# Cross-attention scores: two heads as 128 stationary columns instead of one head as 64

## The chip, the cores and the metric

One core of a Trainium2 chip runs the whole kernel in one launch. The metric is the device time of an execution in microseconds (us); lower is better. Times before and after are medians over executions. One execution was also recorded by the hardware profiler, and all rows below come from that one.

## The reference

One pre-norm decoder layer on 32 sequences of 64 tokens, 512 wide, all in float32: `x = x + self_attention(norm(x))`, `x = x + cross_attention(norm(x), ctx)`, `x = x + lora_linear(norm(x))`. Only the second step is touched. It has 32 query heads of 128 in 8 groups; the four query heads of a group share one key head and one value head:

```python
q = (query @ Wq).reshape(nb, q_len, H, D).transpose(0, 2, 1, 3)     # nb 32, q_len 64, H 32, D 128
k = (key @ Wk).reshape(nb, q_len, KVH, D).transpose(0, 2, 1, 3)     # KVH 8
v = (value @ Wv).reshape(nb, q_len, KVH, D).transpose(0, 2, 1, 3)
q = q * cos + _rotate_half(q) * sin
k = k * cos + _rotate_half(k) * sin
k = jnp.repeat(k, GROUPS, axis=1)                                   # GROUPS 4
v = jnp.repeat(v, GROUPS, axis=1)
scores = jnp.einsum('bhqd,bhkd->bhqk', q, k) / jnp.sqrt(jnp.float32(D))
scores = jnp.where(mask == 0, jnp.float32(-1000000000.0), scores)
attn = jax.nn.softmax(scores, axis=-1)
x = jnp.einsum('bhqk,bhkd->bhqd', attn, v)
return x.transpose(0, 2, 1, 3).reshape(nb, q_len, H * D) @ Wo
```

## The kernel before

The program is written engine by engine: each engine has its own list of work, in program order, and semaphores (`need`) tie the lists together. There is no planner; the order is the order of the code. Keys and values of the cross-attention are computed first and parked in device memory, then self-attention runs (to about 515 us), then cross-attention (about 515 to 1350 us), then the LoRA linear layer.

Cross-attention (`CrossAttention`) walks over `ITS` = 32 iterations: 8 groups of heads, and within each group 4 blocks of 512 tokens (8 sequences). One iteration is one group of four query heads (`h` = 0 to 3) on one block. `product3` (L68, matmuls at L75 to L77) and `output` (L1233 to L1235) build an accurate product out of three fast products (`F32R`, operands split into a high and a low part). The scores (L1194) and the transposes (L1205) are done on plain float32; a plain float32 product is recorded as two weight loads (LDWEIGHTS) and two matmuls.

TensorE's own list in the steady loop of `rest()` is, for iteration `it`: `mix(it, 0)`, `mix(it, 1)` (attention times values, L1220), `scores(it + 1)` (L1194), `queries(it + 2, 0)` (L75 to L77, 12 matmuls), `output(it, 0)` (L1233 to L1235, 12 matmuls), `queries(it + 2, 1)`, `output(it, 1)`, `turn(it + 1, 0)` (4 transposes, L1205), `queries(it + 2, 2)`, `turn(it + 1, 1)`, `queries(it + 2, 3)`, `output(it, 2)`, `output(it, 3)`.

What the scores need and who waits for them:

- VectorE (DVE) `rotate(it, h)` applies the rotary embedding to one head's queries with `rotate_terms` (L169 to L171): the cosine term goes into `q_rot`, the sine term into `rb`. GpSimd (POOL) `add_terms` (L1583) adds `rb` into `q_rot`. `scores` waits for all four heads of its iteration (`q_added`).
- `scores` takes, for each of the 8 sequences of the block and each of the four heads, the 64 queries of that head as the stationary operand (128 rows, 64 columns) and the 64 keys as the moving operand. Heads 0 and 2 write result partitions 0 to 63, heads 1 and 3 partitions 64 to 127: the two halves of the array's columns. That is 32 products an iteration.
- DVE `shift` (L1427, L1430, L1432) then masks and subtracts the maximum, ScalarE (ACT) takes the exponential, DVE sums and inverts (`invert`, L1437, L1440), POOL normalises (`normalise_p`, L1576), and `turn` (L1205) transposes the result. In DVE's list `rotate(it + 2, 0)` and `add(it, 0)` stand between `shift(it + 1)` and `invert(it + 1)`; in POOL's list `add_terms(it + 2, 0)` stands ahead of `normalise_p(it + 1, ...)`.
- At the first iteration of each group but the first, ACT splits four new output weights (`split_o_hi`, L1155) once the outputs of the last group are done, and POOL makes their low parts (`split_o_lo`, L1159); `output(it, 0)` waits for them, head by head (`ready["o"]`).
- DVE `outputs_lo` (L1464) writes 64-element runs that lie 128 elements apart, because `o_lo` is laid out with two sequences side by side.

The score loop of before:

```python
for h in range(H):
    rows = slice(h % PAIR * SEQ, (h % PAIR + 1) * SEQ)
    mm = nc.tensor.matmul(ps_s[half][rows, (h // PAIR * UB + j) * SEQ:(h // PAIR * UB + j + 1) * SEQ],
                          q_rot[:, h, cols], k_t[:, cols], start=True, stop=True)
```

Of the kernel before, what the change touches and what calls it, by code (L numbers as in the profile page):

```python
# [22 lines left out]
ALU = mybir.AluOpType  # L23
# [3 lines left out]
P = 128  # L27
BATCH, SEQ, HIDDEN = 32, 64, 512
TOKENS = BATCH * SEQ
TILES = TOKENS // P  # L30
BLOCK = 512
# [10 lines left out]
H2, KVH, D2 = 32, 8, 128  # L42
HPG2 = H2 // KVH
HALF = D2 // 2
# [9 lines left out]
def need(engine, semaphore, value):  # L54

    if not isinstance(value, int) or value > 0:
        engine.wait_ge(semaphore, value)
# [109 lines left out]
def rotate_terms(nc, ps, cos, sin, a, b):  # L167

    nc.vector.tensor_tensor(a[:, :], ps[:, :], cos, ALU.mult)  # L169
    nc.vector.tensor_tensor(b[0:HALF, :], ps[HALF:D2, :], sin[HALF:D2], ALU.mult)  # L170
    return nc.vector.tensor_tensor(b[HALF:D2, :], ps[0:HALF, :], sin[0:HALF], ALU.mult)  # L171
# [860 lines left out]
class CrossAttention:  # L1032


    def __init__(self, nc, m, base, banks, prior, x, norm2, norm3, ident, drams, linear_drams):
        mask_dram, cos_scr, sin_scr, wq_dram, wo_dram, k_scr, v_scr = drams
        SCALE = 1.0 / float(np.sqrt(np.float32(D2)))
        ITS, H = KVH * NB, HPG2
        PRIOR_ITS = G1 * NB
        PAIR, HALVES = 2, 2  # L1040
        UT = TPB // HALVES
        UB = UT * P // SEQ
# [4 lines left out]
        def sb(name, at, shape, dt=F32):  # L1047
            return nc.alloc_sbuf_tensor_at("p4_" + name, shape, dt, offset=base + at * KB)

        xt_hi, xt_lo = sb("xt_hi", 0, [P, KC, TOKENS], F32R), sb("xt_lo", 32, [P, KC, TOKENS], F32R)  # L1050
        cos_t, sin_t = sb("cos_t", 64, [P, TOKENS]), sb("sin_t", 72, [P, TOKENS])
# [6 lines left out]
        rb = sb("rb", 104, [P, BLOCK])  # L1058
        o_hi, o_lo = (sb(n, at, [P, TPB, H, 2, SEQ], F32R) for n, at in (("o_hi", 106), ("o_lo", 150)))
        bound = sb("bound", 114, [P, BATCH, SEQ])  # L1060
        k_t, v_in = sb("k_t", 122, [P, BLOCK]), sb("v_in", 124, [P, BLOCK])
        v_hi, v_lo = sb("v_hi", 126, [P, BLOCK], F32R), sb("v_lo", 128, [P, BLOCK], F32R)
        s = sb("s", 130, [P, COLS, SEQ])
        xn = [sb(f"xn{i}", 150 + 2 * i, [P, HIDDEN]) for i in range(2)]
        q_rot = sb("q_rot", 158, [P, H, BLOCK])
        pt_hi, pt_lo = (sb(n, at, [P, TPB, H * SEQ], F32R) for n, at in (("pt_hi", 166), ("pt_lo", 170)))
        mx, total, inv = (m.sb(n, [P, COLS]) for n in ("mx", "total", "inv"))
        offset = m.sb("offset", [P, TILES])
        ps_s, ps_o, ps_free_q, ps_free_y = banks

        ps_p = ps_s
        ps_q = [ps_free_q, ps_o[0], ps_free_q, ps_o[2]]
        ps_y = [ps_free_y, ps_o[1], ps_o[3], ps_free_y]

        def tile_bank(t):

            return ps_s[t % 2] if t < 2 * TPB else ps_o[1 + 2 * (t % 2)]
# [7 lines left out]
        q_done, q_terms, q_added = m.sem("q_done"), m.sem("q_terms"), m.sem("q_added")  # L1085
# [13 lines left out]
        def tokens(it):  # L1099
            return slice(it % NB * BLOCK, (it % NB + 1) * BLOCK)  # L1100
# [45 lines left out]
        def split_q_lo(pool, g, h):  # L1146
            need(pool, part_hi["q"], 4 * g + h + 1)
            nc.gpsimd.tensor_tensor(w_lo["q"][h][:, :], raw[h][:, :], w_hi["q"][h][:, :], ALU.subtract).then_inc(ready["q"], 1)
# [8 lines left out]
        def split_o_lo(pool, g, h):  # L1157
            need(pool, part_hi["o"], 4 * g + h + 1)
            nc.gpsimd.tensor_tensor(w_lo["o"][h][:, :], raw[h][:, :], w_hi["o"][h][:, :], ALU.subtract).then_inc(ready["o"], 1)  # L1159

        def tensor(pe):
# [20 lines left out]
            def scores(it):  # L1182

                if it >= ITS:
                    return
                need(pe, q_added, (it + 1) * H)
                need(pe, k_in, (it + 1) * 16)
                need(pe, pt_ready, 2 * it)
                for half in range(HALVES):
                    for j in range(UB):  # L1190
                        cols = slice((half * UB + j) * SEQ, (half * UB + j + 1) * SEQ)
                        for h in range(H):
                            rows = slice(h % PAIR * SEQ, (h % PAIR + 1) * SEQ)
                            mm = nc.tensor.matmul(ps_s[half][rows, (h // PAIR * UB + j) * SEQ:(h // PAIR * UB + j + 1) * SEQ],  # L1194
                                                  q_rot[:, h, cols], k_t[:, cols], start=True, stop=True)
                mm.then_inc(s_done, 1)

            def turn(it, half):
# [48 lines left out]
            def rest():  # L1247
                queries(1, 0)
                scores(0)
                queries(1, 1)  # L1250
                for t in range(2 * TPB, 3 * TPB):
# [7 lines left out]
                for it in range(LAST - 1):  # L1259
                    mix(it, 0)  # L1260
                    mix(it, 1)
                    scores(it + 1)
                    queries(it + 2, 0)
                    output(it, 0)
                    queries(it + 2, 1)
                    output(it, 1)
                    turn(it + 1, 0)
                    queries(it + 2, 2)
                    turn(it + 1, 1)
                    queries(it + 2, 3)  # L1270
                    output(it, 2)
                    output(it, 3)
                mix(LAST - 1, 0)
                mix(LAST - 1, 1)
                scores(LAST)
                output(LAST - 1, 0)
                output(LAST - 1, 1)
# [138 lines left out]
        def vector(dve):  # L1416
# [25 lines left out]
            def rotate(it, h):  # L1442
                if it >= ITS:
                    return
                k = it * H + h
                need(dve, q_done, k + 1)
                need(dve, q_added, k)
                need(dve, s_done, it)
                if k == 0:
                    need(dve, tables_in, 32)  # L1450
                    need(dve, prior["p_norm"], PRIOR_ITS * 4)
                if k == 2:
                    need(dve, prior["pv_done"], PRIOR_ITS)
                rotate_terms(nc, ps_q[h], cos_t[:, tokens(it)], sin_t[:, tokens(it)], q_rot[:, h, :], rb).then_inc(q_terms, 1)

            def turned_lo(it, half):
                need(dve, pt_part, 2 * it + half + 1)
# [40 lines left out]
            def rest():  # L1498
                need(dve, masked, 2)
                shift(0)  # L1500
                rotate(1, 0)
                tile_parts_lo(8)
                tile_parts_lo(9)
                invert(0)
                rotate(1, 1)
                for t in range(10, 13):
                    tile_parts_lo(t)
# [62 lines left out]
        def gpsimd(pool):  # L1570
            def normalise_p(it, half):
                if it >= ITS:
                    return
                need(pool, p_inv, it + 1)
                part = s[:, half * SETS:(half + 1) * SETS, :]
                nc.gpsimd.tensor_tensor(part, part, inv[:, half * SETS:(half + 1) * SETS].unsqueeze(2).broadcast_to([P, SETS, SEQ]),  # L1576
                                        ALU.mult).then_inc(p_norm, 1)

            def add_terms(it, h):
                if it >= ITS:  # L1580
                    return
                need(pool, q_terms, it * H + h + 1)
                nc.gpsimd.tensor_tensor(q_rot[:, h, :], q_rot[:, h, :], rb[:, :], ALU.add).then_inc(q_added, 1)  # L1583

            def values_lo(it):
                if it >= ITS:
                    return
                need(pool, v_part, it + 1)
                nc.gpsimd.tensor_tensor(v_lo[:, :], v_in[:, :], v_hi[:, :], ALU.subtract).then_inc(v_ready, 1)  # L1589

            def rest():
                for h in range(H):
                    add_terms(0, h)
                for h in range(H):
                    split_o_lo(pool, 0, h)
                values_lo(0)
                add_terms(1, 0)
                add_terms(1, 1)
                normalise_p(0, 0)
                normalise_p(0, 1)  # L1600
                add_terms(1, 2)
                add_terms(1, 3)
                for it in range(LAST):
                    g, b = it // NB, it % NB
                    if b == 0 and g > 0:
                        for h in range(H):
                            split_o_lo(pool, g, h)
                    values_lo(it + 1)
                    add_terms(it + 2, 0)
                    normalise_p(it + 1, 0)  # L1610
                    normalise_p(it + 1, 1)
                    if b == 1 and g + 1 < KVH:
                        split_q_lo(pool, g + 1, 0)
                    add_terms(it + 2, 1)
                    if b == 1 and g + 1 < KVH:
                        split_q_lo(pool, g + 1, 1)
                    add_terms(it + 2, 2)
                    if b == 1 and g + 1 < KVH:
                        split_q_lo(pool, g + 1, 2)
                    add_terms(it + 2, 3)  # L1620
                    if b == 1 and g + 1 < KVH:
                        split_q_lo(pool, g + 1, 3)
                lin.zero_b(pool)
                for n in range(LB):
                    lin.add_bias(pool, n)

            return lambda g, h: split_q_lo(pool, g, h), rest
# [331 lines left out]
```

## Time and profile before

| | us |
|---|---|
| median of 2 executions | 1440.48 (1439.39 to 1441.57) |
| the profiled execution, its own time | 1439.55 |
| its span, first to last instruction | 1437.8 |
| granted TensorE clock over the span | 0.995 of full speed |

PE is TensorE's matmuls, PEld its weight loads, which the profile lists apart and which may overlap matmuls. A matmul's recorded duration includes its way through the array, so matmuls that follow one another overlap in the records; the distance between starts tells what one costs. "Idle before" is the time an engine stood still ahead of an instruction, and the name behind the arrow is what ended it.

### The profile page before, as it was taken

What the parts mean: (1) busy time and instruction counts of PE and PEld (TensorE: products, weight loads), DVE (VectorE), ACT (ScalarE), POOL (GpSimd) and SP (SyncE); (2) the same over time, 40 slices, a digit from 0 to 9 for tenths busy, and PEclk for the clock granted to TensorE, in tenths of its full rate; (3) what the DMA queues carried; (4) which work ended last, traced back from release to release, by engine and by line L of the source; (5) the groups of instructions that cost most, each with busy time, mean ns of one, the idle gap of its engine ahead of it and who ended that gap; (6) DMA issues with size and microseconds to landing.
All of it is one profiled execution on the core that took longest, in us unless ns stands there. A gap on an engine that the chain in (4) does not pass through costs nothing.

```text
span 1437.8 us, 27956 instructions
## 1 busy us (share of the span) xinstructions
PE 1397.0 (97%) x11616; PEld 1155.3 (80%) x11616; DVE 1020.9 (71%) x1470; ACT 430.1 (30%) x731; POOL 527.5 (37%) x459
## 2 busy tenths in 40 slices
PE   7999999999997889999999999999999999999999
PEld 6788888788886678888888888888888888888787
DVE  3655552789889877777777777777767767778754
ACT  4211233656657422122123122122122122121421
POOL 4322220433443434344344344344344344342231
PEclk9999999999999999999999999999999999999999
DMA  8565330000005201011011011011012011003011
GB/s 250 169 205 183 104 103 1 3 17 25 10 3 147 59 16 45 30 45 46 30 45 46 29 45 53 22 45 59 16 45 60 16 45 59 16 16 115 1 59 59
DMA packets 79116, 84.09 MB, mean 58 GB/s; under 512 B 9824, under 2 KB 50928, under 8 KB 78736
## 3 DMA queue, kind: packets, MB, share of 16 engines
q1 hardware_dynamic: 68976, 63.42, 13.9%
q10 hardware_dynamic: 9216, 16.78, 3.7%
q0 software_dynamic: 800, 2.11, 0.6%
q8 instruction: 94, 1.54, 0.4%
q14 instruction: 30, 0.25, 0.1%
HBM read 59.22 MB, written 23.07 MB: 57 GB/s over the span
## 4 chain that ended last, share of the span: by engine, by line
PE 85%; DVE 5%; POOL 4%; issue 2%; ACT 2%; DMA 1%; another core or an unknown queue 0%; SPq 0%; ACTq 0%; DVEq 0%
PE p_ps_qk L75 6%; PE p_ps_qk L77 6%; PE p_ps_qk L76 6%; PE p_ps_y L1233 6%; PE p_ps_y L1234 6%; PE p_ps_y L1235 6%; PE p_ps_s L75 5%; PE p_ps_s L76 5%; PE p_ps_s L77 5%; PE p_ps_s L1194 3%; POOL p_wo_lo L1159 3%; PE p_ps_o L75 3%; PE p_ps_o L76 3%; PE p_ps_o L77 3%; PE p_ps_s L1220 2%
## 5 line engine op out<-in xcount | busy, mean ns | idle before, releaser
L1583 POOL TENSOR_TENSOR p_q_rot<-p_q_rot,p_rb 128x512 f32<-128x512 f32 x128 | 165.6, 1294 | 331.7 <-DVE p_rb L171 331.7
L1233 PE MATMUL p_ps_y<-p_wo_hi,p_o_hi 128*128 128x512 f32 x384 | 151.0, 393 | 1.9 <-DVE p_o_lo L1464 1.3
L1234 PE MATMUL p_ps_y<-p_wo_lo,p_o_hi 128*128 128x512 f32 x384 | 149.4, 389 | 0.0
L1235 PE MATMUL p_ps_y<-p_wo_hi,p_o_lo 128*128 128x512 f32 x384 | 149.4, 389 | 0.0
L75 PE MATMUL p_ps_qk<-p_xt_hi,p_wq_hi 128*128 128x512 f32 x312 | 130.4, 418 | 1.5 <-issue 1.0
L77 PE MATMUL p_ps_qk<-p_xt_hi,p_wq_lo 128*128 128x512 f32 x312 | 122.9, 394 | 0.0
L1000 POOL TENSOR_TENSOR p_pn<-p_p,p_inv 128x512 f32<-128x512 f32 x64 | 66.2, 1066 | 154.2 <-DVE p_inv L890 151.6
L76 PE MATMUL p_ps_qk<-p_xt_lo,p_wq_hi 128*128 128x512 f32 x312 | 121.9, 391 | 0.0
L1473 DVE TENSOR_TENSOR x_sb<-p_ps_y,x_sb 128x512 f32<-128x512 f32 x96 | 66.4, 691 | 70.6 <-PE p_ps_y L1235 69.6
L1332 ACT ACTIVATE p_pt_hi<-p_ps_s 128x512 fp32r<-128x512 f32 x64 | 38.1, 599 | 255.3 <-PE p_ps_s L1205 255.2
L1338 ACT ACTIVATE p_o_hi<-p_ps_s 128x512 fp32r<-128x512 f32 x64 | 34.8, 595 | 242.8 <-PE p_ps_s L1220 242.8
L1233 PEld LDWEIGHTS p_ps_y<-p_wo_hi,p_o_hi 128*128 128x128 f32 x384 | 72.1, 188 | 20.0 <-POOL p_wo_lo L1159 3.6
L304 POOL TENSOR_TENSOR p_k_out<-p_k_out,p_rb 128x512 f32<-128x512 f32 x32 | 44.9, 1402 | 115.8 <-DVE p_rb L171 115.8
L1589 POOL TENSOR_TENSOR p_v_lo<-p_v_in,p_v_hi 128x512 fp32r<-128x512 f32 x32 | 42.4, 1325 | 114.0 <-ACT p_v_hi L1323 114.0
L1235 PEld LDWEIGHTS p_ps_y<-p_wo_hi,p_o_lo 128*128 128x128 f32 x384 | 72.1, 188 | 15.0
L1234 PEld LDWEIGHTS p_ps_y<-p_wo_lo,p_o_hi 128*128 128x128 f32 x384 | 72.1, 188 | 14.8 <-issue 0.2
L1576 POOL TENSOR_TENSOR p_s<-p_s,p_inv 128x512 f32<-128x512 f32 x64 | 65.6, 1046 | 35.6 <-DVE p_inv L1440 35.6
L169 DVE TENSOR_TENSOR p_q_rot<-p_ps_qk,p_cos_t 128x512 f32<-128x512 f32 x64 | 43.8, 685 | 42.1 <-PE p_ps_qk L77 42.1
L75 PEld LDWEIGHTS p_ps_qk<-p_xt_hi,p_wq_hi 128*128 128x128 f32 x312 | 58.9, 189 | 13.9 <-issue 2.1
L77 PEld LDWEIGHTS p_ps_qk<-p_xt_hi,p_wq_lo 128*128 128x128 f32 x312 | 58.7, 188 | 13.8
L1194 PE MATMUL p_ps_s<-p_k_t,p_q_rot 128*64 128x64 f32 x2048 | 66.8, 224 | 2.2 <-POOL p_q_rot L1583 2.2
L1327 ACT ACTIVATE p_s<-p_s 128x1024 f32<-128x1024 f32 x32 | 34.0, 1062 | 114.6 <-DVE p_s L1432 114.6
(262 smaller groups left out, 3794.0 us busy)
## 6 DMA issues: line engine op xcount, KB each, us to landing
v_scratch<-p_v_out SPq DMA_DIRECT2D x32, 256.0 KB
k_scratch<-p_k_out SPq DMA_DIRECT2D x32, 256.0 KB, 2.1
p_raw<-in_wq SPq DMA_DIRECT2D x32, 256.0 KB, 3.0
p_raw<-in_wo SPq DMA_DIRECT2D x32, 256.0 KB, 2.6
p_k_t<-k_scratch ACTq DMA_DIRECT2D x32, 256.0 KB, 2.6
p_v_in<-v_scratch ACTq DMA_DIRECT2D x32, 256.0 KB, 2.8
x_sb<-in_x SPq DMA_DIRECT2D x16, 256.0 KB, 2.9
out<-p_y SPq DMA_DIRECT2D x16, 256.0 KB, 2.0
```

The costliest lines, as they stand in the source:

```text
L75: nc.tensor.matmul(out, lh, rh, start=(c == 0), stop=False)
L76: nc.tensor.matmul(out, lh, rl, start=False, stop=False)
L77: mm = nc.tensor.matmul(out, ll, rh, start=False, stop=(c == last))
L304: nc.gpsimd.tensor_tensor(k_out[i % 2][:, :], k_out[i % 2][:, :], rb[i % 2][:, :], ALU.add).then_inc(k_added, 1)
L1000: nc.gpsimd.tensor_tensor(pn[:, u * PB:(u + 1) * PB, :, :].rearrange("p b j k -> p j b k"), part, scale.unsqueeze(3).broadcast_to([P, HALF ...
L1194: mm = nc.tensor.matmul(ps_s[half][rows, (h // PAIR * UB + j) * SEQ:(h // PAIR * UB + j + 1) * SEQ], q_rot[:, h, cols], k_t[:, cols], star ...
L1233: nc.tensor.matmul(ps_y[t][:, :], oh, w_hi["o"][h][:, :], start=(h == 0), stop=False)
L1234: nc.tensor.matmul(ps_y[t][:, :], oh, w_lo["o"][h][:, :], start=False, stop=False)
L1235: mm = nc.tensor.matmul(ps_y[t][:, :], ol, w_hi["o"][h][:, :], start=False, stop=(h == H - 1))
L1473: nc.vector.tensor_tensor(x[:, tile, :], ps_y[t][:, :], x[:, tile, :], ALU.add).then_inc(y_added, 1)
L1576: nc.gpsimd.tensor_tensor(part, part, inv[:, half * SETS:(half + 1) * SETS].unsqueeze(2).broadcast_to([P, SETS, SEQ]), ALU.mult).then_inc( ...
L1583: nc.gpsimd.tensor_tensor(q_rot[:, h, :], q_rot[:, h, :], rb[:, :], ALU.add).then_inc(q_added, 1)
```

## The change

Two heads become one stationary operand. `q_rot` is laid out so that for each pair of heads and each sequence the 64 queries of both heads lie side by side, 128 contiguous columns, and one matmul of 128 rows by 128 columns computes both heads' scores. An iteration then has 16 products in place of 32; each still moves 64 columns of keys. The results land in the same places of `ps_s`. `rotate` writes its cosine term, and `add_terms` reads and writes `q_rot`, in runs of 64 elements that lie 128 apart; the sine terms are as before. No wait is added or removed, and no instruction of DVE, ACT, POOL or the DMA queues.

```diff
-        q_rot = sb("q_rot", 158, [P, H, BLOCK])
+        q_rot = sb("q_rot", 158, [P, H // PAIR, BLOCK // SEQ, PAIR, SEQ])
...
+        def by_batch(rows):
+
+            return rows.rearrange("p (b q) -> p b q", q=SEQ)
...
-                        cols = slice((half * UB + j) * SEQ, (half * UB + j + 1) * SEQ)
-                        for h in range(H):
-                            rows = slice(h % PAIR * SEQ, (h % PAIR + 1) * SEQ)
-                            mm = nc.tensor.matmul(ps_s[half][rows, (h // PAIR * UB + j) * SEQ:(h // PAIR * UB + j + 1) * SEQ],
-                                                  q_rot[:, h, cols], k_t[:, cols], start=True, stop=True)
+                        b = half * UB + j
+                        for i in range(H // PAIR):
+                            mm = nc.tensor.matmul(ps_s[half][:, (i * UB + j) * SEQ:(i * UB + j + 1) * SEQ],
+                                                  q_rot[:, i, b, :, :].rearrange("p r q -> p (r q)"), k_t[:, b * SEQ:(b + 1) * SEQ], start=True, stop=True)
...
-                rotate_terms(nc, ps_q[h], cos_t[:, tokens(it)], sin_t[:, tokens(it)], q_rot[:, h, :], rb).then_inc(q_terms, 1)
+                nc.vector.tensor_tensor(q_rot[:, h // PAIR, :, h % PAIR, :], by_batch(ps_q[h][:, :]), by_batch(cos_t[:, tokens(it)]), ALU.mult)
+                nc.vector.tensor_tensor(rb[0:HALF, :], ps_q[h][HALF:D2, :], sin_t[HALF:D2, tokens(it)], ALU.mult)
+                nc.vector.tensor_tensor(rb[HALF:D2, :], ps_q[h][0:HALF, :], sin_t[0:HALF, tokens(it)], ALU.mult).then_inc(q_terms, 1)
...
-                nc.gpsimd.tensor_tensor(q_rot[:, h, :], q_rot[:, h, :], rb[:, :], ALU.add).then_inc(q_added, 1)
+                rotated = q_rot[:, h // PAIR, :, h % PAIR, :]
+                nc.gpsimd.tensor_tensor(rotated, rotated, by_batch(rb[:, :]), ALU.add).then_inc(q_added, 1)
```

## Rows read from the trace of the kernel before

**Rows 1.** Page, busy time: us (share of the span), instructions.

```profile
PE 1397.0 (97%) x11616; PEld 1155.3 (80%) x11616; DVE 1020.9 (71%) x1470; ACT 430.1 (30%) x731; POOL 527.5 (37%) x459
```

**Rows 2.** Page, the chain that ended last, by engine.

```profile
PE 85%; DVE 5%; POOL 4%; issue 2%; ACT 2%; DMA 1%; another core or an unknown queue 0%; SPq 0%; ACTq 0%; DVEq 0%
```

**Rows 3.** Busy time by window: an ordinary iteration, and a group's first one.

```profile
core 0: us, PE busy (x) PEld busy (x) DVE busy (x) ACT busy (x) POOL busy (x), PEclk, DMA share, GB/s
...
568.19:594.82 26.63, 26.63 (x193) 22.16 (x193) 19.79 (x28) 4.84 (x8) 8.46 (x7) 1.00 0.10 30
942.14:969.15 27.01, 26.92 (x193) 22.08 (x192) 19.95 (x28) 6.92 (x12) 14.49 (x11) 1.00 0.21 59
```

**Rows 4.** The score line: duration ns min/median/max; rows*columns of the stationary operand.

```profile
L1194 PEld LDWEIGHTS p_ps_s<-p_k_t,p_q_rot x2048: 132/138/138, 487.5 to 1320.0; 128*64 128x64 f32 x187
L1194 PE MATMUL p_ps_s<-p_k_t,p_q_rot x2048: 222/222/271, 487.5 to 1320.1; 128*64 128x64 f32 x187
```

**Rows 5.** Timeline (start, us) of one score stretch, in windows growing from 917.127.

```profile
917.13 0.13 PEld L1194 LDWEIGHTS p_ps_s<-p_k_t,p_q_rot 128*64 128x64 f32 x1
...
917.13 0.14 PEld L1194 LDWEIGHTS p_ps_s<-p_k_t,p_q_rot 128*64 128x64 f32 x2
...
917.13 0.19 PEld L1194 LDWEIGHTS p_ps_s<-p_k_t,p_q_rot 128*64 128x64 f32 x3
...
917.13 0.28 PE L1194 MATMUL p_ps_s<-p_k_t,p_q_rot 128*64 128x64 f32 x2
...
917.13 2.09 PE L1194 MATMUL p_ps_s<-p_k_t,p_q_rot 128*64 128x64 f32 x64
...
919.14 0.19 PEld L75 LDWEIGHTS p_ps_qk<-p_xt_hi,p_wq_hi 128*128 128x128 f32 x1
919.25 0.19 PEld L76 LDWEIGHTS p_ps_qk<-p_xt_lo,p_wq_hi 128*128 128x128 f32 x1
```

**Rows 6.** Plain float32 at other widths: loads of 32 and 128 columns.

```profile
L641 PEld LDWEIGHTS p_ps_o<-p_pt,p_v_x x1024: 106/110/178, 271.4 to 467.9; 128*32 128x32 f32 x171
...
L1835 PEld LDWEIGHTS p_ps_s<-p_pick,p_la x16: 190/190/190, 1328.4 to 1333.3; 128*128 128x128 f32 x16
L1835 PE MATMUL p_ps_s<-p_pick,p_la x16: 379/379/379, 1328.6 to 1333.6; 128*128 128x256 f32 x16
```

**Rows 7.** Timeline of L1835's start, windows growing from 1326.7.

```profile
1326.77 0.19 PEld L1835 LDWEIGHTS p_ps_qk<-p_pick,p_la 128*128 128x128 f32 x1 [1.18 <-DVE p_pick L1777]
...
1326.77 0.30 PEld L1835 LDWEIGHTS p_ps_qk<-p_pick,p_la 128*128 128x128 f32 x2 [1.18 <-DVE p_pick L1777]
...
1326.77 1.56 PE L1835 MATMUL p_ps_qk<-p_pick,p_la 128*128 128x256 f32 x6 [0.76 <-DVE p_pick L1777]
```

**Rows 8.** Transposes: loads of 128 float32 columns, and four of them in time.

```profile
L1205 PEld LDWEIGHTS p_ps_s<-ident,p_s x256: 138/140/142, 511.6 to 1334.4; 128*128 128x128 f32 x128
...
930.18 0.60 PE L1205 MATMUL p_ps_s<-ident,p_s 128*128 128x128 f32 x4
```

**Rows 9.** Waits, 515 to 1320 us: total us, times, longest.

```profile
PEld p_ps_y L1233 <- POOL p_wo_lo L1159: 3.6, 7, 0.5
```

**Rows 10.** Lines, shapes apart: busy us, mean ns, idle before.

```profile
L1464 DVE TENSOR_TENSOR p_o_lo<-p_ps_s,p_o_hi 128x512 fp32r<-128x512 f32 x64 | 41.2, 686 | 25.1 <-ACT p_o_hi L1338 24.9
...
L169 DVE TENSOR_TENSOR p_q_rot<-p_ps_qk,p_cos_t 128x512 f32<-128x512 f32 x64 | 43.8, 685 | 42.1 <-PE p_ps_qk L77 42.1
...
L1583 POOL TENSOR_TENSOR p_q_rot<-p_q_rot,p_rb 128x512 f32<-128x512 f32 x128 | 165.6, 1294 | 331.7 <-DVE p_rb L171 331.7
```

**Rows 11.** Timeline of the normalising and the first transposes behind it.

```profile
928.49 2.05 POOL L1576 TENSOR_TENSOR p_s<-p_s,p_inv 128x512 f32<-128x512 f32 x2 [0.84 <-DVE p_inv L1440]
...
929.95 0.58 PEld L1205 LDWEIGHTS p_ps_s<-ident,p_s 128*128 128x128 f32 x4
```

**Rows 12.** Window (us, PE busy, PEclk, DMA share, GB/s), and timeline just before.

```profile
498.50:500.00 1.50, 1.50 (x6) 0.50 0.00 0
...
496.61 0.91 PE L163 MATMUL p_ps_s<-ident,p_xn 128*128 128x128 f32 x4 [3.16 <-DVE p_xt_lo L1488]
```

## The prediction

> **What bounds the kernel now.** I read the page's busy times first: matmuls stand at 97% of the span, and the next engine, DVE, at 71% [rows 1]. The chain that ended last agrees, with 85% of the time on PE [rows 2]. An average hides stages, so I then took the stage that is touched, by windows of one iteration. An ordinary iteration takes 26.63 us and PE is busy for all 26.63; DVE is at 19.79 and POOL at 8.46 [rows 3]. In cross-attention, then, TensorE's list is the time: what an iteration's PE work gains or loses reaches the end, 32 times over. The one exception in the loop is a group's first iteration, at 27.01 us [rows 3]: there the output product waits for the split weights from POOL, 3.6 us in 7 waits [rows 9].
>
> **What a score stretch costs now.** The line has 2048 recorded matmuls, 64 in each of 32 iterations, two for each of 32 products [rows 4]. They take 2.01 us: the first load starts at 917.13 and the next product's load (L75) at 919.14 [rows 5]. How those 64 share the time decides everything. In the windows that are cut off later and later, the second load starts 0.01 after the first (0.14 against 0.13 for the end), the third only after 0.05 (0.19 less its own 0.14) [rows 5]. So two loads, for the two halves of the array's columns, run side by side, and the two matmuls as well (both end by 0.28). The last matmul ends at 2.09 and lasts 0.222 [rows 4, 5], so it starts at 1.87; with 0.055 for the first load this leaves 31 slots in 1.815, that is 0.0585 for a *pair*. The stretch is 0.055 + 31 x 0.0585 + 0.14, where the last term is the pause before L75's load. Heads that the code writes one after the other already run at the same time. The change cannot save what is already shared.
>
> **What the new stretch costs.** 16 products, still two loads and two matmuls each: 32 slots, as many as there are pairs now. A slot costs the longer of its load and its matmul, if the one hides behind the other.
>
> The load: recorded loads of plain float32 last 110, 138 and 190 ns at 32, 64 and 128 columns [rows 4, 6]. The fixed part is equal, and 64 more columns add 52, 32 fewer take off 28: about 0.83 ns a column, so some 0.053 for 64 columns and 0.107 for 128. The rows confirm both from the side: the third half-width load starts 0.05 after the first [rows 5], the second full-width load 0.11 after the first (0.30 less 0.19) [rows 7].
>
> The matmul: L1835 is the same kind of product, full array and plain float32. Six of its matmuls end at 1.56; less one duration of 0.38 and the first load of 0.11, five intervals of 0.214 remain for 256 columns [rows 6, 7], thus 0.054 for 64 columns. At half width load and matmul were balanced (0.053 and 0.054); at full width the load doubles while the matmul stays, and the matmul no longer hides it.
>
> So a slot is a load of 0.108 and what a pair's slot has beyond its load, 0.0585 - 0.055, some 0.004: I take 0.112. Bounds: 0.109, the interval of the full-width transposes ((0.60 - 0.272) / 3 [rows 8]), and 0.117, twice a pair's slot. The pause of 0.14 before L75 I count as gone: at L1835, which follows itself at full width, the next load starts where the matmul before it starts streaming [rows 7], and L75 is full width as well; if it stays, it costs 32 x 0.14 = 4.5 us. The new stretch is then 32 x 0.112 = 3.58 us, 1.57 more than 2.01. Over 32 iterations that is **+50.2 us**. By the bounds: 32 x (3.49 - 2.01) = +47.4, and 32 x (3.74 + 0.14 - 2.01) = +59.8.
>
> **What lies beside it.** The 7 group starts get something back. POOL's split of the output weights hangs on the outputs of the group before, not on the scores, so its end stays where it is, while PE now arrives 1.57 later. Their excess of 27.01 - 26.63 = 0.38 is covered: 7 x 0.38 = **-2.7 us**; the bound is 0, should POOL start later for a reason I don't see.
>
> DVE's cosine term and POOL's addition now touch 64-element runs 128 apart. The trace has such a store on DVE: `outputs_lo` writes that very pattern and takes 686 ns, where the cosine term in its old layout takes 685 [rows 10]. I count zero. POOL has no row for it; its addition takes 1294 ns [rows 10] and I count zero again. The cover: after the scores, POOL's first normalising ends at 928.49 + 1.02 = 929.51, and the first transpose's load starts at 929.95 [rows 11], so 0.44 us are spare; DVE's extra comes out of these, POOL's first out of the 0.84 in which it waited for DVE [rows 11]. Below zero I see no reason to go; above, should DVE's term double (+0.69), 0.25 an iteration would show, +8 us. That the scores come later harms nobody: DVE, ACT and POOL have more idle time in a longer iteration, and the softmax chain and the work that covers it on PE move back together.
>
> **The sum.** +50.2 - 2.7 = +47.5 us. On the profiled execution's own 1439.55 that gives 1487.0; the median of the runs shown lies 0.9 above that execution, so I say **1488**. Its own bounds are 1440.5 + 47.4 - 2.7 = 1485 and 1440.5 + 59.8 = 1500.
>
> **The rivals.**
>
> *Not slower: a full-width load costs no more than a half-width one.* This has a row in its favour. The transposes load 128 float32 columns and show 140 ns, hardly more than the 138 of 64 columns [rows 4, 8]. Were score loads like that, a slot would be the matmul's, some 0.0585 with its overhead; the stretch would be 32 x 0.0585 = 1.87, less than now by the pause, and the time 1440.5 - 32 x 0.14 = 1436, within 2%. It decides as soon as a full-width load is shorter than 0.063 (2.01 / 32). Against it stand L1835's loads, which are plain float32 in an ordinary product, as the new ones: 190 ns, and 0.11 apart [rows 6, 7]. The Trainium skill has the rule that one might hope for here: "TensorE: Matmul & The Clock Gate", section "Weight-path perf modes — Fast Weight Load (FWL) and DoubleRow", says that a faster load comes on by itself at exactly 128 weights, but not for FP32. By that rule the loads stay long; L1835's 190 ns agrees.
>
> *Much slower: loads don't hide at all.* If a full-width load waits for the matmul before it, a slot is 0.108 + 0.054 = 0.162, the stretch 5.18, and the time 1440.5 + 32 x 3.17 - 2.7 = 1539. For it: nothing in rows of this shape, as no full-array float32 product here is shorter than its load. Against it: at L1835 five intervals of 0.214 hold a matmul of 0.214 and a load of 0.108 each [rows 7], so the load was hidden. The same page of the Trainium skill, section "Part 3: Packing small matmuls — row/col tiling", states that loads overlap with matmuls in flight only where they address other rows of the array. By that rule this rival would hold, as all rows are used; the rows of L1835 speak against it.
>
> *Much slower: the clock falls.* With matmuls streaming only half of the time in the stretch, the granted clock could drop. It stood at half speed in one place that I looked at, 498.5 to 500.0, and what went before was 3.16 us without any matmul [rows 12]. The new stretch has no such gap. If it fell after each stretch for the 1.5 us of that row, half of these would be lost: 32 x 0.75 = 24 us more, 1512; with the whole new stretch at half speed too, 32 x 3.58 = 115 more, 1603.
>
> *The change doesn't do what it says:* were the 128 columns still loaded as two halves, the time would stay at about 1440; the count of loads (32 or 64 an iteration) would show it. No row speaks for it; it goes with the first rival.
>
> **How the numbers follow.** My forecast has 0.84. The first rival, with the last, has 0.06; loads that don't hide 0.04; the clock 0.04. A gain of over 2% would need a stretch of 1.1 us, below 32 matmuls of 0.054 (1.73): no row allows it, and I leave 0.02 for what I can't see. About 2% (29 us) is what a measurement of this kernel can tell from no change, and even the low bound of +44.7 lies beyond it: slower 0.92, same 0.06, faster 0.02. The range goes a little past the forecast's bounds, for a load that is a touch shorter and for the spread of runs: 1480 to 1503; it leaves out the rivals, with 0.16.
>
> **What would show it.** In the new profile: 32 score loads an iteration of about 190 ns, matmuls still near 222, starting 0.112 apart one by one; a stretch of 3.6 us; no pause before L75; iterations of about 28.2 us, group starts no longer than the others; no wait of L1233 on POOL; PE still busy throughout, and DVE terms near 0.69. I'm wrong if loads show 140 ns or start 0.06 apart (first rival), if they start 0.16 apart (second), if the clock in the stretch or behind it is below 1.00 (third), or if PE idles before the transposes (DVE or POOL slowed by the strides).

## The result, and the profile after

The kernel after takes 1492.61 us (median of two executions, 1491.64 and 1493.58), the kernel before 1440.48: a ratio of 1.0359 with an interval of 1.0342 to 1.0376. The forecast was 1488 with a range of 1480 to 1503, and slower. The profiled execution after took 1493.58 us with a span of 1491.8; against the one before that is +54.0.

The page of the kernel after, busy times and the chain by engine:

```profile
PE 1450.3 (97%) x10592; PEld 1210.8 (81%) x10592; DVE 1025.0 (69%) x1470; ACT 429.9 (29%) x731; POOL 518.1 (35%) x459
...
PE 86%; DVE 9%; issue 3%; POOL 1%; ACT 1%; DMA 1%; SPq 0%; DVEq 0%; ACTq 0%
```

There are 1024 fewer matmuls than in [rows 1] and 53 us more busy time on PE: fewer instructions, more time. POOL is 9 us *less* busy; that small number comes back below.

The score line after (L1197), duration ns min/median/max:

```profile
L1197 PEld LDWEIGHTS p_ps_s<-p_k_t,p_q_rot x1024: 186/192/335, 488.1 to 1374.0; 128*128 128x128 f32 x171
L1197 PE MATMUL p_ps_s<-p_k_t,p_q_rot x1024: 275/275/422, 488.1 to 1374.1; 128*128 128x64 f32 x171
```

Half as many loads as in [rows 4], 192 ns each in place of 138. The load of 128 columns costs what L1835's did [rows 6]. The matmuls record 275 rather than 222; what a product costs is how far apart they start, and that shows in the loads' starts in the timeline of one stretch after, in windows that grow from 577.978 (start, us):

```profile
577.97 0.19 PEld L1197 LDWEIGHTS p_ps_s<-p_k_t,p_q_rot 128*128 128x128 f32 x1
...
577.97 0.30 PEld L1197 LDWEIGHTS p_ps_s<-p_k_t,p_q_rot 128*128 128x128 f32 x2
...
577.97 0.41 PEld L1197 LDWEIGHTS p_ps_s<-p_k_t,p_q_rot 128*128 128x128 f32 x3
...
577.97 3.65 PEld L1197 LDWEIGHTS p_ps_s<-p_k_t,p_q_rot 128*128 128x128 f32 x32
...
581.54 0.19 PEld L75 LDWEIGHTS p_ps_qk<-p_xt_hi,p_wq_hi 128*128 128x128 f32 x1
```

The ends go 0.19, 0.30, 0.41: one load after another, 0.11 apart. The last of 32 starts at 3.65 - 0.19 = 3.46, so a slot is 3.46 / 31 = 0.1116. The stretch to L75's load takes 581.54 - 577.97 = 3.57, and L75's load comes 0.11 after the last score load: the pause of [rows 5] is gone.

Windows of the kernel after: an ordinary iteration, a group's first one, and the first score stretch of all, at the start of cross-attention.

```profile
core 0: us, PE busy (x) PEld busy (x) DVE busy (x) ACT busy (x) POOL busy (x), PEclk, DMA share, GB/s
...
576.36:604.55 28.19, 28.19 (x163) 23.79 (x162) 19.78 (x28) 4.84 (x8) 8.46 (x7) 1.00 0.09 28
632.73:661.31 28.58, 28.40 (x163) 23.71 (x162) 20.49 (x28) 6.91 (x12) 13.46 (x11) 1.00 0.18 56
...
488.15:494.30 6.15, 6.15 (x31) 6.15 (x32) 0.00 (x0) 0.69 (x1) 6.03 (x5) 0.54 0.46 132
```

Against [rows 3]: the ordinary iteration has +1.56, and PE is busy for all of it. A group's first one is still 0.39 longer than the others, which was to vanish. And the first stretch took over 6 us at a mean granted clock of 0.54. The same stretch in the kernel before, window (us, PE busy, PEclk, DMA share, GB/s):

```profile
487.55:489.40 1.85, 1.85 (x63) 1.00 0.03 9
```

That was 1.85 at full clock. Windows from the second score stretch to the last, 30 iterations, of the kernel before and of the kernel after (us, PE busy, PEclk, DMA share, GB/s):

```profile
516.57:1318.24 801.67, 801.06 (x5762) 1.00 0.12 38
...
521.61:1370.58 848.97, 846.96 (x4802) 1.00 0.12 36
```

In two more profiled executions of the kernel after, from the runs below, this stretch took 848.96 and 848.95: the loop repeats to a few hundredths, and what differs between these executions lies ahead of it.

The span's +54.0 is 32 x 1.56 = 49.9, some 0.4 from the group starts (six are 0.33 to 0.39 over an ordinary iteration and the last one 1.08, 3.2 in all, where before's seven made 2.7), 3.5 for a later start of cross-attention (0.6 ahead of its first score stretch, 2.9 in its first iteration), and 0.2 in the last iterations.

### The profile page after: what moved, and what is told of

Same layout as the page of the kernel before. It is cut to its first block, busy times and chain, and to the rows that moved or that the text cites. A ratio compares the mean times of both kernels' runs of the same rounds, so it can differ in the third digit from the quotient of the medians.

```text
span 1491.8 us, 25908 instructions
## 1 busy us (share of the span) xinstructions
PE 1450.3 (97%) x10592; PEld 1210.8 (81%) x10592; DVE 1025.0 (69%) x1470; ACT 429.9 (29%) x731; POOL 518.1 (35%) x459
## 4 chain that ended last, share of the span: by engine, by line
PE 86%; DVE 9%; issue 3%; POOL 1%; ACT 1%; DMA 1%; SPq 0%; DVEq 0%; ACTq 0%
PE p_ps_s L1197 8%; PE p_ps_qk L75 6%; PE p_ps_qk L77 6%; PE p_ps_qk L76 5%; PE p_ps_y L1236 5%; PE p_ps_y L1237 5%; PE p_ps_y L1238 5%; PE p_ps_s L75 5%; PE p_ps_s L76 5%; PE p_ps_s L77 5%; PE p_ps_o L75 2%; PE p_ps_o L76 2%; PE p_ps_o L77 2%; PE p_ps_s L1208 2%; PE p_ps_s L1223 2%
## 5 line engine op out<-in xcount | busy, mean ns | idle before, releaser
L1236 PE MATMUL p_ps_y<-p_wo_hi,p_o_hi 128*128 128x512 f32 x384 | 150.2, 391 | 1.3 <-DVE p_o_lo L1469 1.3
L75 PE MATMUL p_ps_qk<-p_xt_hi,p_wq_hi 128*128 128x512 f32 x312 | 129.7, 416 | 0.9 <-issue 0.9
L1197 PE MATMUL p_ps_s<-p_k_t,p_q_rot 128*128 128x64 f32 x1024 | 124.0, 280 | 2.2 <-POOL p_q_rot L1589 2.2
L1197 PEld LDWEIGHTS p_ps_s<-p_k_t,p_q_rot 128*128 128x128 f32 x1024 | 119.5, 195 | 6.7 <-POOL p_q_rot L1589 2.6
L77 PE MATMUL p_ps_qk<-p_xt_hi,p_wq_lo 128*128 128x512 f32 x312 | 122.8, 393 | 0.0
L1430 DVE TENSOR_TENSOR p_s<-p_ps_s,p_bound 128x512 f32<-128x512 f32 x64 | 41.2, 686 | 84.4 <-PE p_ps_s L1197 84.4
L1236 PEld LDWEIGHTS p_ps_y<-p_wo_hi,p_o_hi 128*128 128x128 f32 x384 | 72.1, 188 | 16.6 <-DVE p_o_lo L1469 1.5
```

What stands on the lines that cost most here:

```text
L75: nc.tensor.matmul(out, lh, rh, start=(c == 0), stop=False)
L77: mm = nc.tensor.matmul(out, ll, rh, start=False, stop=(c == last))
L1197: mm = nc.tensor.matmul(ps_s[half][:, (i * UB + j) * SEQ:(i * UB + j + 1) * SEQ], q_rot[:, i, b, :, :].rearrange("p r q -> p (r q)"), k_t[ ...
L1236: nc.tensor.matmul(ps_y[t][:, :], oh, w_hi["o"][h][:, :], start=(h == 0), stop=False)
```

## The experiments

The first ones go to the main term, what sets a slot; the later ones to what it left over.

### Half-width products in the new layout

```diff
-mm = nc.tensor.matmul(ps_s[half][:, <i, j>], q_rot[:, i, b, :, :].rearrange("p r q -> p (r q)"), k_t[:, <b>], ...)
+for r in range(PAIR):
+    mm = nc.tensor.matmul(ps_s[half][r * SEQ:(r + 1) * SEQ, <i, j>], q_rot[:, i, b, r, :], k_t[:, <b>], ...)
```

(Here and below, names in <> stand for slices that stay as they were.)

> The changed kernel's layout of the queries and its strided DVE and POOL accesses, but the products again as 32 half-width ones side by side. Theory (the load of a full-width stationary operand sets the slot): pairs start 0.058 to 0.059 apart again, the stretch is 2.0 us, the time is that of before, 1440 us (1437 to 1443). Rival (the strided accesses of DVE and POOL cost the time): it stays near 1490.

1440.3 us against 1440.73 of before in the same runs: 0.9992 (0.9969 to 1.0016). Window of this kernel (columns as for the kernel after), an ordinary iteration:

```profile
571.05:597.68 26.63, 26.63 (x194) 22.16 (x194) 19.79 (x28) 4.83 (x8) 8.47 (x7) 1.00 0.09 30
```

The iteration is back at 26.63, to the hundredth. DVE's and POOL's strided accesses, which this kernel keeps, cost nothing (DVE 19.79, POOL 8.47, as in [rows 3]). All of the loss in the loop lies in the form of the product.

### More moving columns under the same loads

Of the 16 products, 12 move two sequences' keys, 128 columns; the surplus results are overwritten by the next product.

```diff
-for j in range(UB):
-    b = half * UB + j
-    for i in range(H // PAIR):
+for i in range(H // PAIR):
+    for j in range(UB):
+        b, n = half * UB + j, 1 if j == UB - 1 else 2
...
-        ... k_t[:, b * SEQ:(b + 1) * SEQ]
+        ... k_t[:, b * SEQ:(b + n) * SEQ]
```

> The changed kernel with 12 of an iteration's 16 products moving 128 key columns in place of 64; the surplus columns are overwritten by the product that owns them. Theory (load of 0.107 us sets the slot, the matmul hides in it; 128 columns need 0.107 too): slots stay near 0.112, the time within 5 us of the changed kernel's 1492. Rival (the matmul, or a load that does not hide, sets the slot): 24 slots an iteration longer by 0.054, 32 x 1.3 = 41 us, 1534.

1491.7 us, ratio 1.0353 (1.0315 to 1.0391), where the kernel after had 1493.95 and 1.0374 in the same runs: nothing got longer. Its score line:

```profile
L1197 PEld LDWEIGHTS p_ps_s<-p_k_t,p_q_rot x1024: 186/192/338, 486.0 to 1372.0; 128*128 128x128 f32 x171
L1197 PE MATMUL p_ps_s<-p_k_t,p_q_rot x1024: 222/275/580, 486.0 to 1372.1; 128*128 128x128 f32 x128, 128*128 128x64 f32 x43
```

Three quarters of the matmuls stream twice as long and the time stays, with the iteration at 28.19. So the matmul is hidden under the load and the load alone sets the slot; loads that didn't hide would have added the longer matmul.

### Fewer moving columns

32 of the 64 keys are moved, so half of the scores are left out.

```diff
-ps_s[half][:, at:at + SEQ], ..., k_t[:, b * SEQ:(b + 1) * SEQ]
+ps_s[half][:, at:at + SEQ // 2], ..., k_t[:, b * SEQ:b * SEQ + SEQ // 2]
```

> The changed kernel with each product moving only the first 32 of its 64 key columns, so that half of the scores are left out. Theory (the load alone sets the slot): slots stay near 0.112, the time within 3 us of the changed kernel's 1492. Rival (load and matmul add up, or the matmul sets the slot): slots shorter by 0.027, 32 x 32 x 0.027 = 27 us less, 1465.

1513.77 us (1513.5 to 1514.04), 1.0506 of before (1.0467 to 1.0544): *slower* by some 20 for less work, which nobody expected. Timeline of this kernel, a score stretch, and a product shortly behind it:

```profile
579.04 3.65 PEld L1197 LDWEIGHTS p_ps_s<-p_k_t,p_q_rot 128*128 128x128 f32 x32
...
582.61 0.19 PEld L75 LDWEIGHTS p_ps_qk<-p_xt_hi,p_wq_hi 128*128 128x128 f32 x1
...
584.58 0.63 PE L77 MATMUL p_ps_qk<-p_xt_hi,p_wq_lo 128*128 128x512 f32 x1
```

The stretch is again 3.57, so as to the slot the theory holds, and the rival (the matmul counts) falls. Windows of this kernel (us, PE busy, PEclk, DMA share, GB/s) show where the rest went:

```profile
579.15:582.70 3.55, 3.55 (x33) 1.00 0.02 7
583.10:586.40 3.30, 3.30 (x10) 0.50 0.00 0
586.50:605.60 19.10, 19.10 (x89) 1.00 0.09 27
...
611.00:614.40 3.40, 3.40 (x24) 1.00 0.00 0
```

Behind the stretch the granted clock stands at 0.50, the level of 1.2 GHz, for the 3.30 us of that window, in which the products of L75 to L77 run; behind the next stretch it stays at 1.00. It falls behind 14 of the 31 stretches that follow the first one; 13 of these iterations are some 1.6 us longer, one 2.0. From the second stretch to the last this kernel takes

```profile
520.68:1390.52 869.84, 868.71 (x4802) 0.97 0.12 35
```

which is 20.9 more than the kernel after, about the whole difference. The prediction's third rival is thus a real mechanism, but not one of this change: in the steady loop of the kernel after, with 64 columns moved, the granted clock is 1.00 throughout.

### The kernel after once more

> The changed kernel as it is, beside the others on one chip. Expected 1492 us (1490 to 1495), and again a first score stretch at half clock (6.2 us); if that was an accident of one execution, the first stretch is 3.6 us and the time 1489 to 1490.

1493.95 us (1491.83 to 1498.77), 1.0374 (1.0337 to 1.0411). The first stretch took 4.7 to the next product's load, between both values that had been expected. The loss at the start is no fixed amount; it comes up again below.

### One column half after the other

Before's half-width products, with the products of one half of the columns gathered, so that neighbours no longer differ in half.

```diff
+for r in range(PAIR):
     for j in range(UB):
-        for h in range(H):
+        for h in range(r, H, PAIR):
```

> The kernel before with the order of its 32 half-width products changed: for each bank of results first the 16 of the one column half, then the 16 of the other, so that neighbours never fall on different halves. Same instructions, same operands. Theory (the kernel before was as fast as it was because neighbours ran side by side): 64 slots of 0.0585 in a row, a stretch of 3.8 to 3.9 us, 57 to 61 us more than before, 1497 to 1501, even a little more than the changed kernel. Rival (a half-width load and matmul take 0.029 each by themselves): no change, 1440.

1477.73 us, 1.0261 (1.024 to 1.0281). Timeline of this kernel, one stretch:

```profile
546.69 3.27 PEld L1195 LDWEIGHTS p_ps_s<-p_k_t,p_q_rot 128*64 128x64 f32 x64
546.69 3.41 PE L1195 MATMUL p_ps_s<-p_k_t,p_q_rot 128*64 128x64 f32 x64
```

The order alone costs 37 us: the same 64 loads of 64 columns that took 2.01 [rows 5] now take over 3.2. Windows of this kernel (columns as for the kernel after), an ordinary iteration and a group's first one:

```profile
602.52:630.43 27.91, 27.91 (x194) 23.49 (x193) 19.78 (x28) 4.84 (x9) 8.45 (x7) 1.00 0.06 20
...
630.43:658.34 27.91, 27.91 (x194) 23.48 (x192) 19.78 (x28) 6.92 (x13) 14.51 (x11) 1.00 0.20 58
```

The iteration is 1.28 longer than before's, and a group's first one is no longer than the others (six of the seven; the last has 0.20 more), which the next experiment needs. So it was the alternation of the two halves that made two products one slot. The expected 3.8 to 3.9 was too high: inside a half the starts are 58 ns apart, but at each of the three changes of half the first products of the new half run beside the last of the old one (9 slots saved; 55 x 0.058 = 3.2). Right in kind, then, and too high by those overlaps.

### POOL's split held back

In the kernel after, at group starts, POOL's split of the values waits until DVE's subtraction is done.

```diff
 # POOL, ahead of values_lo(it + 1)
+if b == 0 and g > 0:
+    need(pool, s_shifted, it + 2)
```

> The changed kernel, and at the first iteration of each later group POOL makes the low part of the values only after DVE has subtracted the maximum. Theory (the wait that took the place of the one on the output weights comes from DVE and POOL working on SBUF operands at the same time: DVE's subtraction takes 2.03 in place of 1.23 us there, and the transposes come late): the subtraction is back at 1.23, the six group starts come down from 28.53 to 28.19 and the last from 29.27 to about 28.4, 2.9 us less in all, 1489 to 1490. Rival (POOL is late because the split weights keep it busy): group starts stay at 28.5.

1488.55 us (1487.65 to 1489.81), 1.0336 (1.032 to 1.0352). Windows of this kernel (columns as for the kernel after), the second a group's first iteration:

```profile
602.65:630.83 28.18, 28.18 (x161) 23.77 (x160) 19.78 (x28) 4.84 (x8) 8.45 (x7) 1.00 0.05 20
630.83:659.01 28.18, 28.18 (x161) 23.78 (x160) 19.77 (x28) 6.91 (x12) 13.48 (x11) 1.00 0.19 57
```

The group starts have lost their excess, as the theory had it; of the last one's 1.08, 0.30 is left. The intervals of this ratio and of the kernel after's (1.0342 to 1.0376) overlap, so that the times alone would not show it; the loop does, from the second score stretch to the last:

```profile
519.71:1365.80 846.09, 845.91 (x4802) 1.00 0.12 36
```

That is 2.9 less than the kernel after's 848.97. What it rests on is one instruction, in the timelines of a group start, first of the kernel after:

```profile
635.43 5.01 POOL L1163 TENSOR_TENSOR p_wo_lo<-p_raw,p_wo_hi 128x512 fp32r<-128x512 f32 x4 [4.23 <-ACT p_wo_hi L1159]
640.40 1.30 POOL L1595 TENSOR_TENSOR p_v_lo<-p_v_in,p_v_hi 128x512 fp32r<-128x512 f32 x1
...
640.75 2.03 DVE L1435 TENSOR_TENSOR p_s<-p_s,p_mx 128x1024 f32<-128x1024 f32 x1
...
649.29 0.42 PEld L1208 LDWEIGHTS p_ps_s<-ident,p_s 128*128 128x128 f32 x4 [0.60 <-POOL p_s L1581]
```

then of the one with the wait:

```profile
638.85 1.23 DVE L1435 TENSOR_TENSOR p_s<-p_s,p_mx 128x1024 f32<-128x1024 f32 x1
...
640.15 1.30 POOL L1595 TENSOR_TENSOR p_v_lo<-p_v_in,p_v_hi 128x512 fp32r<-128x512 f32 x1 [1.62 <-DVE p_s L1435]
```

of the kernel before:

```profile
944.84 6.04 POOL L1159 TENSOR_TENSOR p_wo_lo<-p_raw,p_wo_hi 128x512 fp32r<-128x512 f32 x4 [4.23 <-ACT p_wo_hi L1155]
...
948.47 1.25 DVE L1432 TENSOR_TENSOR p_s<-p_s,p_mx 128x1024 f32<-128x1024 f32 x1
```

and of the one with the half-columns gathered, whose scores come 1.3 later than before's, not 1.56:

```profile
636.45 1.22 DVE L1433 TENSOR_TENSOR p_s<-p_s,p_mx 128x1024 f32<-128x1024 f32 x1
...
636.47 2.37 POOL L1590 TENSOR_TENSOR p_v_lo<-p_v_in,p_v_hi 128x512 fp32r<-128x512 f32 x1
```

Read the durations of DVE's subtraction (L1435, L1432, L1433) and of the POOL operation beside it. Where DVE's subtraction starts while POOL still works, POOL's *next* operation waits: before, the four splits take 6.04 rather than 5.01; with the halves gathered, the split of the values takes 2.37 rather than 1.30, since DVE began 0.02 earlier. Where POOL's operation begins first and still runs when DVE's begins, DVE waits: after, 2.03 rather than 1.23. The Trainium skill has this rule ("SBUF — State Buffer", section "SBUF: two separate sides"): a DVE operation with two SBUF inputs and a GpSimd operation that reads SBUF share a port pair, and whichever starts first holds it for the whole instruction. These rows agree; an estimate by it has DVE wait until POOL's split ends at 641.70, 0.95 us, and 0.80 was measured.

The last group's start has a second part. In the kernel after, DVE's list there also collects a statistic for the next norm (L123) between its addition to `x` and its sum, which it does at no other group's start:

```profile
1325.26 0.69 DVE L123 BATCH_NORM_STATS2 stats<-x_sb 128x6 f32<-128x512 f32 x1
...
1328.53 0.42 PEld L1208 LDWEIGHTS p_ps_s<-ident,p_s 128*128 128x128 f32 x4 [1.31 <-POOL p_s L1581]
```

The 0.36 of the other groups and these 0.69 make 1.05 of the 1.08.

### The first stretch at half width

In the kernel after, only the very first stretch is made of half-width products.

```diff
+if it == 0:
+    <the two products with r of the first experiment>
+else:
     <the product at full width>
```

> The kernel after the change, but with the very first score stretch (iteration 0, the one at the start of cross-attention) made of 32 half-width products; all later iterations stay at full width. Open is why the first stretch of the kernel after took 6.2 us at a mean granted clock of 0.54, where the kernel before took 1.86 at 1.00. Theory: behind the idle time ahead of it, full-width loads with the matmuls between them busy for only half of the time bring the clock to half speed, and half-width products do not (or rarely). Then this first stretch takes 1.9 to 2.0 us at clock 1.00, and the time is 4.3 us below the kernel after of the same runs, about 1488 to 1489. Rival: the clock there depends on the moment, not on the width. Then the first stretch is as likely at half speed, 3.4 us as in the run with half-width products throughout, and the time is 2 to 3 us below the kernel after, 1490 to 1491.

> A second look at the same kernel, since a single execution cannot tell a certain loss from a frequent one. Theory: first stretch again 1.9 to 2.0 us at clock 1.00. Rival: 3.2 to 3.4 us at half speed in some of the looks.

> A third look at the same kernel. Theory: first stretch again 1.9 to 2.0 us at clock 1.00. Rival: 3.2 to 3.4 us at half speed in some of the looks.

> The kernel after, on the same chip and in the same rounds as the one with a half-width first stretch. Theory: its first stretch is slowed again, 4 to 6.2 us, and its median lies 4.3 us above that kernel's. Rival: its first stretch is slowed or not, and the medians lie 2 to 3 us apart.

1489.75 us (1488.38 to 1489.82) with the half-width first stretch, 1492.53 (1487.36 to 1495.05) for the kernel after on the same chip; two more executions with the half-width first stretch took 1491.6 and 1490.74. Windows of the first stretch (us, PE busy, PEclk, DMA share, GB/s), of the first of these executions with a half-width stretch:

```profile
489.20:491.20 2.00, 1.99 (x64) 1.00 0.03 8
```

of the third:

```profile
488.72:492.12 3.40, 3.39 (x64) 0.54 0.26 75
```

and of the kernel after in these runs:

```profile
489.20:494.50 5.30, 5.30 (x32) 0.65 0.39 114
```

The second's first stretch is as the first's. Over all profiled executions, those of the other experiments too, a full-width first stretch ran partly at half speed in 6 of 6 (4.4 to 6.3 us to the next product's load, against 3.57 at full clock), one of narrower products in 2 of 7 (3.4 and 3.5). So neither expectation holds whole: the half-speed clock came with the full width in each execution that was profiled, and it occurs without it.

The times decide nothing here. The medians are 2.8 apart, in the rival's 2 to 3 rather than the theory's 4.3, but the two sets of times overlap, and so do the intervals of their ratios (1.0321 to 1.035, and 1.0333 to 1.0372). One execution of the kernel after that was not profiled took 1487.36 at a mean granted clock of 0.996, where the others in these runs had 0.991 to 0.993: whether its first stretch was slowed at all isn't known. And the first stretch is not all that the clock takes at the start. Windows of the whole first iteration, from the first score stretch to the second, of the kernel before, of the second execution with a half-width first stretch, and of the kernel after (us, PE busy, PEclk, DMA share, GB/s):

```profile
487.54:516.57 29.03, 20.35 (x164) 0.88 0.18 55
...
488.00:519.17 31.17, 22.66 (x164) 0.80 0.17 52
...
488.10:521.61 33.51, 26.35 (x133) 0.75 0.16 47
```

PE stands still for a good part of it, and the clock falls further on in this iteration in every kernel, before's too ([rows 12] lies there). The second execution had its first stretch at full clock and still lost time behind it, 31.17 in place of the first execution's 28.65.

### Four quarters

Before, with each product cut in two of 32 stationary columns.

```diff
-mm = nc.tensor.matmul(ps_s[half][rows, <h, j>], q_rot[:, h, cols], k_t[:, cols], ...)
+for part in range(2):
+    first, at = h % PAIR * SEQ + part * SEQ // 2, cols.start + part * SEQ // 2
+    mm = nc.tensor.matmul(ps_s[half][first:first + SEQ // 2, <h, j>], q_rot[:, h, at:at + SEQ // 2], k_t[:, cols], ...)
```

> The kernel before with each product cut in two of 32 stationary columns, four side by side: twice the products, half the load each. Theory (a slot is the longer of load and matmul; at 64 columns they are equal, at 32 only the matmul counts, and four products share it): a slot of 0.056 as in the self-attention's 32-column products, a stretch 0.08 us shorter, 2 to 3 us less, 1438. Rival (the count of instructions sets the pace): a stretch of up to twice 1.87 us, 1500.

1438.19 us (1436.97 to 1440.59) against 1440.99: 0.9988 (0.9978 to 0.9997), the fastest version of all, if by next to nothing. Timeline of one of its stretches:

```profile
542.95 1.99 PE L1196 MATMUL p_ps_s<-p_k_t,p_q_rot 128*32 128x64 f32 x128
...
544.87 0.50 PE L75 MATMUL p_ps_qk<-p_xt_hi,p_wq_hi 128*128 128x512 f32 x1
```

128 matmuls, twice as many as before, in 1.99 us: four now share a slot of 56 ns, and the iteration is 26.56. A quarter's load is shorter still (some 27 ns, an estimate by the prediction's 0.83 ns a column), so the slot is down to the matmul's 54 and a little, and by that more cutting has nothing left to win; no run tried it. This is the change's opposite, and it points the other way.

## Why the prediction came out as it did

**The slot and the stretch: right.** A slot of 0.112 was predicted, 0.1116 measured; a stretch of 3.58, 3.57 measured; +1.57 an iteration, +1.56 measured. What carried it was to see in [rows 5] that before's products ran in pairs, so that 32 products were only 32 slots, and to take the load of 128 columns from L1835 [rows 6, 7] rather than from the transposes [rows 8]. The gathered halves show the pairing by taking it away, the long and short moving operands that the load alone sets the new slot. One sign missed, without harm to the sum: the matmuls were to record near 222 and record 275.

**The pause before L75, and the strides: right.** The pause went; the kernel with half-width products in the new layout shows that the strides cost nothing, on POOL too, for which there had been no row.

**The group starts, -2.7: wrong.** The failed step is "the softmax chain and the work that covers it on PE move back together", with the claim that POOL's excess is simply covered. The wait of L1236 (before's L1233) on POOL's split of the weights did go; no row of it is left among the waits. But the chain moved back against *POOL's* list, which hangs on the group before. Waits of the kernel after, 520 to 1375 us (total us, times, longest):

```profile
PEld p_ps_s L1208 <- POOL p_s L1581: 5.4, 8, 1.3
```

The transposes now wait where the output product did. DVE's subtraction begins 0.35 after POOL's split of the values and takes 0.80 longer; the 0.44 us that the prediction had found spare ahead of the transposes [rows 11] cover a good half, and 0.36 is left, which is the measured excess of six of the seven. The prediction had named PE idle ahead of the transposes as a sign of being wrong; it came, though not from the strides. The same rows suggest where before's 0.38 came from: POOL's four weight splits took 1.03 longer behind the same subtraction; seven times that is 7.2 of the 9 us that POOL is less busy after. That the expected gain was there to be had is shown twice: with the halves gathered (1.3 later) POOL is the one that waits, and six of the seven group starts are as long as an ordinary iteration; with the split held back, the loop is 2.9 us shorter. The net term was +0.4, not -2.7: 3.1 us of the miss.

**The start of cross-attention: not in the sum.** The prediction counted 32 equal stretches, and its third rival set a falling clock aside because the new stretch has "no such gap" as that of [rows 12]. The first stretch has one: PE's loads waited 2.6 us for POOL's rotated queries, in the kernel before as well.

```profile
488.10 0.19 PEld L1197 LDWEIGHTS p_ps_s<-p_k_t,p_q_rot 128*128 128x128 f32 x1 [2.59 <-POOL p_q_rot L1589]
```

Behind it the stretch ran mostly at the lower level: the third rival's sign, a clock below 1.00 in the stretch, in one stretch of 32. Of the 3.5 us, 0.6 lay ahead of the stretch and is spread between executions (it began at 485.96 to 490.54 in the thirteen that were profiled); the 2.9 in the first iteration is this execution's, and the two others of the kernel after lost less there (31.85 and 31.68 in place of 33.51). Why the full-width stretch there was slowed in each profiled execution and a narrower one only sometimes, the runs don't settle.

**The rivals.** Loads as cheap at 128 columns as at 64: ruled out by 192 ns and 0.11 apart. Columns still loaded as two halves: ruled out by 32 loads an iteration. Loads that don't hide: ruled out by the unchanged time with long moving operands. The rule of the Trainium skill cited in the prediction, that loads overlap only with matmuls on other rows ("TensorE: Matmul & The Clock Gate", "Part 3: Packing small matmuls — row/col tiling"), is not what this chip did here: every product uses all rows, and twice the moved columns in 12 of 16 products left the loads 0.112 apart. The same section of the Trainium skill also lets a load go ahead of matmuls in flight where it goes into a background weight buffer; that would fit these rows, but no run here shows such a buffer. The falling clock: not in this change's steady loop, but in its first stretch, and real with 32 moved columns, at 1.6 us a time and more.

**The sum.** Against the profiled execution +47.5 was predicted and +54.0 measured: 3.1 more from the group starts, 3.5 from the start, 0.2 from the last iterations, -0.3 from the stretch. The median lies 1.0 below that execution, and the forecast of 1488 was 1.0 above its own sum, so that 4.6 remain between the two. The range took them in, but not by foresight: its upper part was meant for a longer slot and a pause that stays, and neither came. That part is luck; the slot, which makes nine tenths of the change, isn't.

## What to carry to other kernels

Before merging small products into a full array, look whether the small ones already run side by side: cut the timeline off later and later and see whether the second load starts with the first or after it. Where a product moves few columns, as the 32 to 128 here, its slot is the load, and a load of 128 columns took twice what one of 64 took; separate column groups then loaded in parallel, and it is their order (neighbours in different groups) that made them do so. And when one chain is moved in time, check it against each list that does not move with it: an operation that met nothing before can come to lie beside one that holds it up.

## What was not expected of the hardware

- Four plain float32 loads of 32 columns, with their matmuls, take 56 ns side by side, hardly less than two of 64 (58 ns); one of 128 takes 112.
- The same 32 products, only reordered by column half, cost 37 us more.
- Moving 32 columns rather than 64 under the same loads made the kernel some 20 us slower, since the granted clock fell to 0.50 behind 14 of the stretches.
- One DVE subtraction of 128x1024 took 2.03 us rather than 1.23 because a POOL operation had begun 0.35 us before it; with DVE 0.02 us ahead, POOL's took 2.37 rather than 1.30.
